# Two sums of squares as neighbouring 32-column matmuls, and their DMA in two halves

## What is computed

```python
Bm = (x @ WB.T).reshape(B_, L, H, N)          # B_ = 4, L = 512, H = 64, N = 128
Cm = (x @ WC.T).reshape(B_, L, H, N)
Bm = rmsnorm(Bm, Bn_w) + B_bias               # x * rsqrt(mean(x * x) + 1e-6) * w
Cm = rmsnorm(Cm, Cn_w) + C_bias
theta = (x @ Wth.T).reshape(B_, L, H, N // 2)
theta_cumsum = jnp.cumsum(theta * dt[..., None], axis=1)
Bm = rope(Bm, theta_cumsum)
Cm = rope(Cm, theta_cumsum)
# then, over the sequence: h = a * h + b * B_prev x_prev + g * B x;  y = C h
```

## Time and profile before

| | us |
|---|---|
| median of 3 runs | 3865.8 |
| lowest and highest run | 3859.18, 3869.25 |
| profiled execution: its own time | not listed by the profile |
| profiled execution: span, first to last instruction | 3597.7 |
| median less span | 268.1 |

### The profile page before, as it was taken

The page is one execution under the profiler, slowest core; times in us unless marked ns, Lnnn a source line. Parts: engine busy times, 40 slices in busy tenths (PEclk is TensorE's granted clock), DMA queues, the critical chain, the costliest instruction groups (busy, mean ns, idle before and its releaser), DMA issues.

```text
span 3597.7 us, 79586 instructions
## 1 busy us (share of the span) xinstructions
PE 3137.4 (87%) x26192; PEld 2498.8 (69%) x26192; DVE 2667.2 (74%) x4086; ACT 1819.1 (51%) x3680; POOL 1747.9 (49%) x1420
## 2 busy tenths in 40 slices
PE   5459986999999989999986999999899999966993
PEld 4348865777777667777764787877577877755882
DVE  5423447999999489999945999998499999742346
ACT  1236554655654365556414666664466666323651
POOL 3730523555555156666610666665065666534066
PEclk7679988999998999999978999999999999988996
DMA  9857856555453255554403555552455555266795
GB/s 389 282 183 253 279 178 179 154 177 183 153 177 117 74 168 145 163 157 144 117 2 109 152 158 166 146 164 72 120 148 164 161 147 164 63 242 211 258 327 181
DMA packets 311252, 613.99 MB, mean 171 GB/s; under 512 B 59136, under 2 KB 159616, under 8 KB 310016
## 3 DMA queue, kind: packets, MB, share of 16 engines
q1 hardware_dynamic: 286464, 544.19, 48.8%
q0 software_dynamic: 24576, 67.14, 5.7%
HBM read 454.67 MB, written 155.45 MB: 170 GB/s over the span
## 4 chain that ended last, share of the span: by engine, by line
PE 46%; DVE 22%; issue 13%; DMA 8%; SPq 3%; ACT 3%; POOL 3%; DVEq 1%; POOLq 0%; ACTq 0%
PE bank L62 10%; PE bank L565 7%; PE bank L578 5%; DVE xbc L1259 5%; PE bank L1370 4%; PE bank L1331 3%; PE bank L1400 3%; DVE tmp L1283 2%; PE bank L556 2%; DMA rr_bc<-rr_dram 2%; DVE rot L1283 2%; DVE xc L1265 2%; PE bank L1192 2%; DMA th_raw<-w_att 2%; POOL xd L489 2%
## 5 line engine op out<-in xcount | busy, mean ns | idle before, releaser
L62 PE MATMUL bank<-xh,wb 128*128 128x512 f32 x2048 | 708.6, 428 | 49.8 <-ACT sqt L1203 26.7
L1200 ACT ACTIVATE xbc<-bank,norm_w 128x512 f32<-128x512 f32 x512 | 350.1, 684 | 560.2 <-PE bank L62 470.1
L1291 POOL TENSOR_TENSOR rot<-rot,tmp 128x512 f32<-128x512 f32 x256 | 332.7, 1299 | 606.6 <-DVE tmp L1283 606.6
L1283 DVE SCALAR_TENSOR_TENSOR tmp<-xbc,bias,cs_sn 128x1024 f32<-128x1024 f32 x256 | 449.3, 1755 | 0.0
L62 PEld LDWEIGHTS bank<-xh,wb 128*128 128x128 f32 x2048 | 359.5, 194 | 125.7 <-ACT sqt L1203 31.7
L1292 POOL TENSOR_TENSOR rot<-rot,tmp 128x512 f32<-128x512 f32 x256 | 437.7, 1710 | 0.0
L641 DVE TENSOR_TENSOR hh<-sg,bank 128x96 f32<-128x96 f32 x384 | 97.7, 254 | 443.1 <-ACT sg L616 375.5
L62 PE MATMUL bank<-xl,wb 128*128 128x512 f32 x1024 | 415.1, 405 | 0.0
L1283 DVE SCALAR_TENSOR_TENSOR rot<-xbc,bias,cs_sn 128x1024 f32<-128x1024 f32 x256 | 375.4, 1466 | 0.1
L1303 POOL TENSOR_TENSOR sq<-cst,rho 128x512 f32<-128x512 f32 x128 | 153.5, 1200 | 363.4 <-DVE x L1011 335.5
L1259 DVE TENSOR_TENSOR xbc<-xbc,rr_bc 128x1024 f32<-128x1024 f32 x256 | 315.5, 1271 | 16.3 <-DMA rr_bc<-rr_dram 15.7
(11 more groups left out here) (258 smaller groups left out, 6535.0 us busy)
## 6 DMA issues: line engine op xcount, KB each, us to landing
wb<-watt_dram SPq DMA_DIRECT2D x96, 1024.0 KB, 6.8
rr_bc<-rr_dram SPq DMA_DIRECT2D x128, 512.0 KB, 6.7
yd<-ys SPq DMA_DIRECT2D x96, 512.0 KB
wd<-w_down SPq DMA_DIRECT2D x384, 96.0 KB
watt_dram<-wb SPq DMA_DIRECT2D x32, 1024.0 KB, 5.4
dt_bc<-row_dram SPq DMA_DIRECT2D x256, 128.0 KB, 2.9
al_bc<-row_dram SPq DMA_DIRECT2D x256, 128.0 KB, 2.9
xd<-xg SPq DMA_DIRECT2D x12, 2048.0 KB, 23.8
```

The lines of the kernel that those rows point to most:

```text
L62: ins = e.matmul(dst, a, m, start=start and c == 0, stop=stop and c == n - 1, skip_group_check=not (start and stop))
L1200: e.activation(xbc[j % 4][:, i, :], XBANK[i % 2][:, :], ACT.Copy, scale=norm_w[:, i:i + 1])
L1283: ins = e.scalar_tensor_tensor(o[:, 2 * ty:2 * ty + 2, :], X[:, i, :].unsqueeze(1).to_broadcast([P, 2, SEQ]), bias_of(i), cs_sn[j % 2][:, ...
L1291: e.tensor_tensor(R[:, 2 * ty, :], R[:, 2 * ty, :], tmp[:, 2 * ty + 1, :], ALU.subtract)
```

## The change

`ss_pe` waits once, for both sums of squares of the pair, then issues the two matmuls behind each other. Each takes a 32-column window of `one_hot` as its stationary matrix and writes 32 partitions of the bank: B's sums into partitions 0 to 31, C's into 32 to 63, of which rows 0 to 3 and 32 to 35 carry values once two pairs are done. The root is taken over partitions 0 to 35. The values to be moved now lie in two blocks of 4 rows, so `R_sp1` issues two DMAs, each from 4 rows to 64 partitions, and the waits on their semaphore count two. The order of the rows changes from pair, type, head to type, pair, head, and the reader at line 1259 follows.

```diff
-        stdr = decay_t[0:8, :, :, :].rearrange("p k q a -> p (k q a)")
+        stdr = decay_t[0:36, :, :, :].rearrange("p k q a -> p (k q a)")
@@ ss_pe
+            first = 6 - 2 * (j % 2)
+            e.wait_ge(e_sqs.sem, e_sqs.at(2 * m + 2))
             for ty in range(2):
-                e.wait_ge(e_sqs.sem, e_sqs.at(2 * m + ty + 1))
-                c = (j % 2) * 2 + ty
-                e.matmul(SSB[:, :], one_hot[:, 6 - 2 * c:6 - 2 * c + P], sqs[:, ty, :],
-                         start=c == 0, stop=c == 3, skip_group_check=True).then_inc(e_ssm.sem, 1)
+                e.matmul(SSB[32 * ty:32 * ty + 32, :], one_hot[:, first:first + 32], sqs[:, ty, :],
+                         start=j % 2 == 0, stop=j % 2 == 1, skip_group_check=True).then_inc(e_ssm.sem, 1)
@@ R_act
-            e.wait_ge(a_r1.sem, a_r1.at(gm))
-            e.activation(stdr, SSB[0:8, :], ACT.Sqrt, scale=1.0 / NS, bias=eps_nm[0:8, 0:1]).then_inc(e_sr.sem, 1)
+            e.wait_ge(a_r1.sem, a_r1.at(2 * gm))
+            e.activation(stdr, SSB[0:36, :], ACT.Sqrt, scale=1.0 / NS, bias=eps_nm[0:36, 0:1]).then_inc(e_sr.sem, 1)
@@ R_dve
-            e.wait_ge(a_r1.sem, a_r1.at(gm + 1))
+            e.wait_ge(a_r1.sem, a_r1.at(2 * (gm + 1)))
@@ R_sp1
-            e.dma_start(rc_in[:, :], stdr.rearrange("r (c w) -> r c w", w=32)).then_inc(a_r1.sem, 16)
+            for ty in range(2):
+                rows = stdr[32 * ty:32 * ty + 4, :].rearrange("r (c w) -> r c w", w=32)
+                e.dma_start(rc_in[CL * ty:CL * ty + CL, :], rows).then_inc(a_r1.sem, 16)
@@ F_dve1
-                r = rr_bc[par][:, (j % 2) * 2 + ty, :]
+                r = rr_bc[par][:, 2 * ty + j % 2, :]
```

## The result

The changed kernel takes 3950.8 us (median), the kernel before 3859.2 us on the same chip: ratio 1.0256, 95% interval 1.0215 to 1.0298. (One execution of the changed kernel, 7351.6 us long at a mean granted clock of 0.432, is left out.) The forecast was 3881 us, slower by 0.4%, and its range ended at 3902. The direction was right, the size wrong by a factor of six (91.6 us against 15).

What follows compares the result with a forecast made beforehand. DVE was taken to bound the pair loop, stalling on the DMA of the roots. DMA costs of 16.1 + 5.2 us less 5 (prologues) and 1 (PE waits) gave +15 us: 3881 us, 0.4% slower, range 3854 to 3902.

Steps and rivals of the forecast that it cites:

- DVE sets the pace, PE waits: Pair loop: DVE needs 16.7 us a turn whatever PE does; PE's saving credited with 1 us for all scans.
- PE waits in 20 of 27 turns: Third scan's pair loop: PE waits for DVE's sums of squares in 20 of 27 turns, so DVE sets the pace.
- The pair overlaps: The two sums' matmuls in each turn: column tiles run side by side, 0.86 us for the pair, saving 0.86 us.
- the switch: Change of array shape between the pair and line 1400: 0.1 us of PE a turn.
- Rival (c): Pair's tiles don't overlap, or only partly; PE becomes the bound, some 36 us, 3905 us in all; chance 0.06.
- The prologues: Start of each scan, pair twice on the path: 2 x 0.75 us saved, 6 us for four scans, 5 taken.
- The DMA: Roots to 128 partitions: two issues, landing 0.67 us later, delaying DVE's reciprocal; costs 16.1 and 5.2 us.
- The clock, rival (b): PE idle near 2 us before the pair halves its clock: 21 us more, 3902 us; chance 0.09.
- the sum 16.1 + 5.2 - 5 - 1: Whole kernel: DMA delays in two kinds of turn, less prologue and PE-wait savings: +15 us.
- Median less span, 268.1 us: Whole kernel: runs' median 3865.8 us lies 268.1 us above the traced span 3597.7; carried over unchanged.
- the signs named ahead: Two issues, stalls 0.7 us longer in all 13, pair about 1.0 us, PE waiting nearly every turn, clock 1.00, prologues shorter.

Runs made afterwards that it cites:

- e7: Kernel before, with only its DMA of the roots issued on SP ahead of the al_bc DMAs: -20.1 us, ratio 0.9947.
- e1: Kernel before, with only its one DMA of 8 rows split into two of four rows: +26.9 us, ratio 1.0049.
- e3: Changed kernel plus one unread 512-column product on PE ahead of the pair's wait: +29.1 us against the kernel before, ratio 1.0071.
- e15: Changed kernel with the unread filler product ahead of the pair's wait, repeated on another chip: +30.5 us against the kernel before, ratio 1.0067.
- e9: 32-column pair with one DMA, plus two spare reciprocals delaying DVE some 0.7 us: +55.2 us against the kernel before, ratio 1.0172.
- e12: 32-column pair with the one DMA of before, repeated on the third chip: +8.9 us against the kernel before, ratio 1.0020.
- e5: Changed kernel's 32-column pair, but rows kept together so one DMA moves them: +9.9 us against the kernel before, ratio 1.0020.
- e4: Changed kernel with the products with the state (`Y2_pe`) issued ahead of the pair: +29.0 us against the kernel before, ratio 1.0086.
- e14: Changed kernel with both of its DMAs issued on SP ahead of al_bc: -24.7 us against the kernel before, ratio 0.9921.
- e0: The changed kernel measured once more, on a second chip: +93.7 us against the kernel before, ratio 1.0242.
- e2: Kernel before with 32-column stationaries only, both sums one after another into partitions 0 to 31: +5.4 us, ratio 1.0002.

## Why the prediction was wrong

- **DVE sets the pace, PE waits**: right in part. e7 confirms that the stall on `rc_in` cost time (taken away, 23 us of the loops are gone). But "PE waits in 20 of 27 turns" was read from the weight loads' row; PE's matmuls stood idle for the sum in 2 turns, 0.8 us, and PE was busy 447.87 of 451.50 us. So PE had next to no slack, and the slack that the change gives it was taken as harmless. At half clock PE is the later one, and in the changed kernel DVE waits for PE, and for ACT behind PE, for 36.4 us in the third scan (16.6 + 13.0 + 6.8) where it waited 1.6.
- **The pair overlaps**: right. Its four passes take 1.05 us, before 1.88, against 0.86 and 0.1 for the switch. Rival (c) is out. The Trainium skill ("TensorE: Matmul & The Clock Gate", Part 3) keeps matmuls in program order. For two tiles of two passes each that would make, by my estimate, three slots of 0.43 us; the 1.05 us has room for little more than two, so here the trace disagrees: in the pair at 1474.54 the four passes start at 1474.54, 1474.54, 1474.99 and 1475.00.
- **The prologues**: the pair fell from 1.72 to 0.98 us. The stretches between the loops as a whole went -1.7, -2.6 and +13.4 us, and they scatter by as much among the experiments, so the 5 us can't be seen.
- **The DMA**: right in price and place. Two issues take 1.26 us in place of 0.69 (forecast 1.37); the median of one is 607 ns (forecast 650). The reciprocal starts 0.66 us later after the first issue (forecast 0.67). The stalls went from 28 to 47 and from 46.2 to 65.3 us; forecast 21 us more, measured 19 here and 22 in e1, 27 us of time with it. The Trainium skill ("DMA: Bandwidth & Descriptors", the rules at its end) advises one transfer, and that is borne out: the halves win nothing. That they hold each other up, as it says, isn't seen here: the second issue starts some 0.65 us after the first (1.26 - 0.61), and from there to the reciprocal it is 2.17 us, as with one DMA (2.16).
- **The clock, rival (b)**: the mechanism was named, given 0.09 and +21 us, and left out of the sum. This is the step that failed: the sum 16.1 + 5.2 - 5 - 1 puts the clock at nothing, because PE's longer wait was taken to cost nothing; measured, 66 us of the 103 on the third chip come only with both parts together, and they go when the clock comes back (e3, e15). Three terms were off. A drop was taken to be 3.4 us as in the earlier trace rows, costing PE 1.7; in the second scan it lasts 10.2 and costs PE, by the same reckoning, half of that, 5.1. It was to decide near 2 us of idle; here 1.14 to 1.26 us in every second turn went ahead of drops. And each drop was priced alone, with PE's slack as cover, where it makes the next: PE late, DVE late, PE idle before the next sum. What is left of each pair of turns was put at 0.5 us; two turns in that chain take 37.5 us against 34.2 (17.8 + 16.4), 3.3 us more, the DMAs included. On the third chip the loss of 102.9 us is 27.9 from the DMAs alone, 8.9 from the pair alone, and 66.1 that only both bring.
- **The parts were summed as if independent.** 28 and 9 us alone, 103 together. Both act on the same gap: the pair makes PE come early, the DMAs make DVE's sum late.
- **Median less span, 268.1 us**: carried over as something around the span; it was the difference between two chips. The two numbers cancel in the forecast, so this cost nothing, but that is luck: it was misread.
- Of the signs named ahead: two issues, longer and more frequent stalls, the pair's length held; the clock at 1.00 didn't, nor did the wait for the sum in nearly all turns (the weight loads' waits went from 20 to 19 of 27; PE's own from 2 to 14).

What stays open: why the change has more and longer low stretches (257 to 335 us) than e9 (160), though DVE is about as late in both. It isn't the number of long waits. In the 90 turns of the three loops PE waits over 1 us ahead of the pair 30 times in the change's first trace, and 29 of these waits have a drop right behind them (one that begins during the wait or within 5 us of its end). In e9 it waits so 28 times, and a drop follows only 14; in e12, 15 of 22. Nor is the length of a wait enough to tell: those of 1.14 to 1.26 us in the second scan all have one behind them, and in e9 four waits of 1.5 to 1.9 us have none. And the slow turns are themselves as long, two by two, as the distance of the drops (37.6 us), in which cause and effect can't be told apart here. So that the stall, the pair and the clock act together is shown, by taking away each in turn (e1, e5, e3, e4, e14); how a wait sets off a drop is not.

## What to carry to other kernels

Time taken off an engine that waits anyway isn't free on PE: look where the new idle time comes to lie, just ahead of a dependent group in every turn, and price a loop of half clock from it, not a single drop. Read an engine's own waits, not those of its weight loads, before you call it idle. Two edits that act on the same wait, one from the early side and one from the late, must be measured together as well as alone. And the cheapest repair stood in the trace of before: a DMA whose source was ready, issued behind one that still waited for DVE. The root is done at 1530.94, SP issues it at 1533.30:

```profile
1530.26 0.68 ACT L1216 ACTIVATE decay_t<-bank,eps_nm 8x512 f32<-8x512 f32 x1
```

Moved ahead, it gave 0.5% to the old kernel and turned the 3% loss of the change into a gain of 0.8%.

## What the runs showed of the hardware

- PE fell to 0.50 for 10.2 us at a time in a loop in which it was busy 96.7% (487.9 of 504.3 us), with idle stretches of 1.14 to 1.26 us ahead of the pair. These 504.3 us hold 136 us at 0.50; e12, with 459.8 of 477.3 us busy (96.3%), has 68. What in the idle time sets a drop off, these runs don't tell.
- The changed kernel got 61 to 74 us faster by an added matmul per turn whose result nobody reads (e3, e15), and nothing else; and with PE as long idle as before, but elsewhere, it lost 29 us in place of 94 (e4, e0).
- One DMA from 8 rows to 128 partitions takes SP 697 ns to issue, each half 607 ns: halving rows and bytes saved 13% of the issue.
- Pairs of 512-column fp32 products in two column tiles run beside each other, both passes: 1.05 us in place of 1.88, the first passes starting within 0.01 us of each other, the second ones too. One behind the other, 32 columns save nothing (e2: 592 ns a product, as with 128).
